# The output stores issued by SyncE instead of GpSimd, in a fused attention and stream-mixing kernel

## The chip, the cores and the metric

The kernel runs on one core of one Trainium2 chip. The metric is the device time of one execution in microseconds (us), as the median of several runs. Less is better.

The names of the engines: PE is TensorE (matrix products), DVE is VectorE, ACT is ScalarE, POOL is GpSimd. SP is SyncE, which computes nothing and only waits for semaphores and issues DMA transfers. POOL can issue DMAs too. A DMA that SP issues goes to the queue that the profile calls q1 (hardware_dynamic), one that POOL issues to q0 (software_dynamic). Both queues are served by the same 16 DMA engines.

## The reference

`x` is (8, 512, 2048) in float32: 8 batches, 512 rows (patches), 2048 columns. Cut to what is computed:

```
def layernorm(x): (x - mean) / sqrt(var + 1e-5)              # over the last axis, 2048
# 1. windowed attention, 8 heads of 32, windows of 128 columns; q and k from x, v from ctx
q, k = Wq @ xn + bq, Wk @ xn + bk;  val = Wv @ ctx + bv       # xn = layernorm(x)
o = softmax(q.T k / sqrt(32), masked) @ val;  out = (Wo @ gelu(o) + bo) * mask
x = x + tanh(g_xattn) * out
# 2. four streams of 512 columns, mixed by small per-row matrices
x1 = layernorm(x);  xr = x1 * rsqrt(mean(x1 * x1) + eps)
H_res  = sinkhorn(xr @ W_res.T + base, 50 iterations)         # 4 x 4 for every row
H_pre, H_post = softmax(xr @ W_pre.T + ..), softmax(xr @ W_post.T + ..)
H_res = (1 - g) * I + g * H_res
y = einsum(x1 streams, H_pre) @ W_branch                      # (rows, 512)
x = x + tanh(g_ffn) * (H_res mixes the four streams of x1 + y * H_post)
```

## The kernel before, in words

One loop counter `g` drives all engines. A step `g` is one attention unit (one window of 128 columns, 128 of the 256 attention channels). Eight steps make a chunk of 512 columns (`UPC` = 8), four chunks a batch (`UNITS` = 32 steps). There are 256 attention steps; the loop runs from -16 to 340, since the stream part of a batch follows its attention part by one to three batches' worth of steps. `G, r = chunk_step(g)` gives the chunk and the place in it. Each engine has its own program: it walks through the same `g` and does at each what tables of offsets say. The order on an engine is fixed by the code; engines meet only through semaphores.

The second part works in two stages. First, for each batch, 49 Sinkhorn iterations in scaling form, two iterations to a step: POOL multiplies `kp = ke * scale` (L526), DVE sums `kp` (L1134) and takes the reciprocal `sa` or `sv` (L1135), and so on back and forth. Then come the batch's four output tiles `t` (128 rows of 2048 columns each), eight steps apart, with step `TILE_AT[t]` as their origin. There are 32 tiles in all. For one tile:

- SP loads the 1 MB row block `x1t` (L385, `load_x1t`), seven steps ahead; there are two such buffers (even, odd). The load waits until the tile two before is complete, which DVE tells by `out_ready`.
- ACT makes the first product of `xpre` (L876), DVE adds the three others (L1167), PE transposes `xpre` (L675), ACT copies it (L884, `xpt`), and PE multiplies it by `W_branch` into bank `f` (L728, eight instructions).
- `otile` (128 x 4 x 512 float32, only one buffer) holds the output. ACT writes its first term for streams 0 and 1 (pair 0) at step -1 and for streams 2 and 3 (pair 1) at step +2 (L893, `first_out`). Before each it waits for `out_stored[pair]`: the store of that half for the tile before must have landed.
- DVE adds three stream products to pair 0 (L1179) at steps 0, 1, 2, then `y` from bank `f` to all four streams at step 3 (L1192, `add_y`, which waits between pair 0 and pair 1 for ACT's pair 1), then three stream products to pair 1 at steps 4, 6 and 7. `out_ready` goes up when pair 0 is complete and again when pair 1 is.
- The two halves are stored to DRAM, 512 KB each, at the end of step +4 and of step +8.

Until about 1660 us the attention of later batches runs beside the tiles of earlier ones. After that only Sinkhorn and tiles are left, and after about 1830 us only the last batch's last tiles.

What else SP does in a chunk of eight steps, in this order: the store of the sum `x1` to `x_dram` (1 MB, L378, waits for POOL's accumulating load to land, at r = 0), statistics loads `xs` (L373), 12 copies into `q_st` (L390, r = 3), more `xs`, the `x1t` load (r = 5), 12 copies into `k_st` and one row (L390, L435, r = 5), then `ctx_raw` (L359), a mask (L362) and `xc` (L356). What else POOL does: `kp`, normalising `xc` (L454), the low parts of `x` and `ctx` (L460, L465), and the accumulating loads into `x1c` (L474).

Of the kernel before, what the change touches and what calls it, by code (L numbers as in the profile page):

```python
# [12 lines left out]
B, D, S = 8, 512, 2048  # L13
# [3 lines left out]
DT = D // P  # L17
# [14 lines left out]
C = S // N  # L32
# [43 lines left out]
def chunk_step(g):  # L76
    return g // UPC, g % UPC


def at_step(g, lead, table):  # L80

    return [((g - r) // UPC - lead, i) for i, r in enumerate(table)
            if (g - r) % UPC == 0 and 0 <= (g - r) // UPC - lead < NG]


def ffn_at(g, e, width=1):

    f = (g - e) // UNITS - 1
    return [f] if (g - e) % UNITS == 0 and 0 <= f < B else []


def tiles_at(g, k):

    return [(f, t) for t in range(DT) for f in ffn_at(g, TILE_AT[t] + k)]


def sink_at(g):

    for f in range(B):
        n = g - UNITS * (f + 1) - SINK_AT  # L100
        if 0 <= n < len(SINK):
            return f, SINK[n]
    return None, (None, None)
# [56 lines left out]
def program(nc, x, ctx4, mask_bc, mask_t, gates, wq_t, bq, wk_t, bk, wv_t, bv, wo_t, bo, wf_t, base,  # L160
            w_branch, ident, stack_i, eye4, out):
    with ExitStack() as ctx:  # L162
        def sb(name, shape, dt=F32):
            return ctx.enter_context(nc.sbuf_tensor(name, shape, dt))
# [4 lines left out]
        def sem(name):  # L169
            return ctx.enter_context(nc.semaphore(name))  # L170
# [74 lines left out]
        otile = sb("otile", [P, N, C])  # L245
# [79 lines left out]
        out_ready = sem("out_ready")  # L325
        out_stored = [sem(f"out_stored{i}") for i in range(2)]
# [6 lines left out]
        outr = out.rearrange("b (t p) s -> b t p s", p=P)  # L333
# [20 lines left out]
        def _(sp):  # L354
# [10 lines left out]
            def load_maskt(b):  # L365
                sp.dma_start(maskt[:, b % 2, :], mask_t[b]).then_inc(maskt_loaded[b % 2], 16)
# [13 lines left out]
            def load_x1t(f, t):  # L380
# [3 lines left out]
                    sp.wait_ge(out_ready, 2 * (n - 1))  # L384
                sp.dma_start(x1t[n % 2][:], x1dr[f, :, t, :]).then_inc(x1t_loaded[n % 2], 16)  # L385

            def stack(G, dst, blocks):
                for r, (src, part) in enumerate(blocks):
                    for h in range(HPT):
                        sp.dma_start(dst[r * DH:(r + 1) * DH, G % 2, :, h, :],  # L390
                                     src[h * DH:(h + 1) * DH, part, :, :]).then_inc(stack_loaded[G % 2], 16)
# [24 lines left out]
            for g in range(FIRST, LAST):  # L416
# [11 lines left out]
                if r == 3 and 0 <= G + 1 < NG:  # L428
                    sp.wait_ge(qk_ready, 4 * (G + 1) + 2)
                    stack(G + 1, q_st, ((q_hl, 0), (q_hl, 1), (q_hl, 0)))  # L430
# [13 lines left out]
                if u == UPC + 6 and g >= 0 and b + 2 < B:  # L444
                    sp.wait_ge(bias_ready, b + 1)
                    load_maskt(b + 2)

        @block.gpsimd
        def _(pool):
            def norm_x(G, t):  # L450
                if t == 0:
                    pool.wait_ge(xc_loaded, 16 * (G + 1))
                    pool.wait_ge(xstat_ready, G // NC + 1)
                nc.gpsimd.tensor_scalar(xc[:, t, :], xc[:, t, :], ra[:, 2, t:t + 1], ra[:, 4, t:t + 1],  # L454
                                        ALU.mult, ALU.add).then_inc(x_norm, 1)

            def split_x(G, t):
                pool.wait_ge(x_norm, DT * G + t + 1)
                pool.wait_ge(x_hi, DT * G + t + 1)
                nc.gpsimd.tensor_tensor(x_hl[:, G % 2, 1, t, :], xc[:, t, :], x_hl[:, G % 2, 0, t, :], ALU.subtract  # L460
                                        ).then_inc(x_split, 1)

            def split_ctx(G, t):
                pool.wait_ge(ctx_hi, DT * G + t + 1)
                ins = nc.gpsimd.tensor_tensor(ctx_hl[:, 1, t, :], ctx_raw[:, t, :], ctx_hl[:, 0, t, :], ALU.subtract)  # L465
                if t == DT - 1:
                    ins.then_inc(ctx_split, 1)

            def add_x(G, h):
                pool.wait_ge(wo_read, DT * G + 2 * h + 2)  # L470
                if G:
                    pool.wait_ge(x1_added[h], 16 * G)
                b = G // NC
                pool.dma_start(x1c[:, 2 * h:2 * h + 2, :], xr[b, :, 2 * h:2 * h + 2, cols(G)],  # L474
                               accum_op=ALU.add).then_inc(x1_added[h], 16)

            def store(f, t, pair):
                pool.wait_ge(out_ready, f * (2 * DT) + 2 * t + pair + 1)
                half = slice(2 * pair * C, 2 * (pair + 1) * C)
                pool.dma_start(outr[f, t, :, half], otile[:, 2 * pair:2 * pair + 2, :].rearrange("p n c -> p (n c)")  # L480
                               ).then_inc(out_stored[pair], 16)

            cp = Chain(pool, pool_chain)

# [6 lines left out]
            def variance(b):  # L491
                pool.wait_ge(mv_a_ready, b + 1)
                nc.gpsimd.tensor_scalar(ra[:, 0, :], mv_a[:, :, 1], LN_EPS, None, ALU.add).then_inc(var_ready, 1)

            def xstat(b):
                pool.wait_ge(var_ready, b + 1)
                pool.wait_ge(rs_act, 2 * b + 2)
                newton(ra[:, 2, :], ra[:, 3, :], ra[:, 0, :], ra[:, 1, :])
                cp.link(nc.gpsimd.tensor_tensor(ra[:, 4, :], mv_a[:, :, 0], ra[:, 2, :], ALU.mult))
                nc.gpsimd.tensor_scalar(ra[:, 4, :], ra[:, 4, :], -1.0, None, ALU.mult).then_inc(xstat_ready, 1)  # L500

            def stat_b(f, part):
                r = rb[:, f % 2]
                if part == 0:
                    pool.wait_ge(mv_b_ready, f + 1)
                    cp.link(nc.gpsimd.tensor_scalar(r[:, 7, :], mv_b[:, :, 0], -1.0, None, ALU.mult))
                    nc.gpsimd.tensor_scalar(r[:, 0, :], mv_b[:, :, 1], LN_EPS, None, ALU.add).then_inc(rs_req, 1)
                elif part == 1:
                    pool.wait_ge(rs_req, 2 * f + 1)
                    pool.wait_ge(rs_done, 4 * f + 2)  # L510
                    newton(r[:, 3, :], r[:, 2, :], r[:, 0, :], r[:, 1, :])
                    cp.link(nc.gpsimd.tensor_tensor(r[:, 6, :], r[:, 7, :], r[:, 3, :], ALU.mult))
                    cp.link(nc.gpsimd.tensor_tensor(r[:, 4, :], r[:, 3, :], r[:, 3, :], ALU.mult))
                    cp.link(nc.gpsimd.tensor_tensor(r[:, 4, :], r[:, 4, :], mv_b[:, :, 1], ALU.mult))
                    nc.gpsimd.tensor_scalar(r[:, 4, :], r[:, 4, :], RMS_EPS, None, ALU.add).then_inc(rs_req, 1)
                else:
                    pool.wait_ge(rs_req, 2 * f + 2)
                    pool.wait_ge(rs_done, 4 * f + 4)
                    newton(r[:, 5, :], r[:, 2, :], r[:, 4, :], r[:, 1, :])
                    nc.gpsimd.tensor_tensor(r[:, 5, :], r[:, 5, :], r[:, 3, :], ALU.mult).then_inc(rb_ready, 1)  # L520
# [7 lines left out]
            def scale_at(f, its, part):  # L528
                it, half = its[part // 2], part % 2
                if (it, half) in SCALED:  # L530
                    scale(f, it, half)
# [5 lines left out]
            for g in range(FIRST, LAST):  # L537
                G, r = chunk_step(g)
                b, u = divmod(g, UNITS)
                f, its = sink_at(g)  # L540
                scale_at(f, its, 0)
                if g >= 0 and u == 17 and b + 1 < B:
                    variance(b + 1)
                if g >= 0 and u == 18 and b + 1 < B:
                    xstat(b + 1)
                for part in range(3):
                    for ready in ffn_at(g, STAT_AT + 1 + part):
                        stat_b(ready, part)
                for H, t in at_step(g, -2, LOW_X_AT):
                    split_x(H, t)  # L550
                scale_at(f, its, 1)
                for H, t in at_step(g, -2, NORM_AT):
                    norm_x(H, t)
                scale_at(f, its, 2)
                for H, t in at_step(g, -1, LOW_CTX_AT):
                    split_ctx(H, t)
                scale_at(f, its, 3)
                if 0 <= G - 1 < NG and r in (6, 7):
                    add_x(G - 1, r - 6)
                for done, t in tiles_at(g, 4):  # L560
                    store(done, t, 0)
                for done, t in tiles_at(g, 8):
                    store(done, t, 1)
            for pair in range(2):
                pool.wait_ge(out_stored[pair], 16 * DT * B)

        @block.tensor
        def _(pe):
# [753 lines left out]
```

## Time and profile before

| | |
|---|---|
| median of 3 runs | 1905.74 us (1904.44 to 1910.57) |
| the profiled execution's own time | 1909.33 us |
| its span | 1907.5 us |
| busy: PE, DVE, ACT, POOL | 1392.2 (73%), 1439.4 (75%), 945.7 (50%), 863.2 (45%) us |
| DMA queue q1 (issued by SP) | 230.41 MB, 39.2% of 16 engines' span |
| DMA queue q0 (issued by POOL) | 67.12 MB, 15.3% |
| stores of the output | 64 of 512 KB, issued by POOL at L480 |

How to read it: the span runs from the first to the last thing that the profile shows; the profiled execution's own time is 1.8 us longer. An engine's share of busy time is an average over stages that are limited by different things, so the stages are read one by one: the stretch with attention (to 1660 us), Sinkhorn with tiles (to 1830 us) and the last tiles (to 1907.5 us).

### The profile page before, as it was taken

The numbers are of one execution on the slowest core, as the hardware profiler recorded it, in microseconds if no ns is written. First come the engines' busy times: TensorE is split into PE (matmuls) and PEld (weight loads), VectorE is DVE, ScalarE is ACT, GpSimd is POOL, SyncE is SP. The second block draws the span as 40 slices with busy tenths as digits, with TensorE's granted clock in tenths as the row PEclk, the third lists the DMA queues.
The fourth block names the chain that finished last, engine by engine and source line by source line (L and its number), as shares of the span: only waits on it lengthen the run. The fifth ranks groups of instructions, "written<-read, shape, count | busy, mean of one in ns | idle before, by whom it ended". The sixth has DMA issues, their size and how long they took to land. (4 is left out here: it accounts for less than half of the span.)

```text
span 1907.5 us, 35318 instructions
## 1 busy us (share of the span) xinstructions
PE 1392.2 (73%) x12301; PEld 849.8 (45%) x12448; DVE 1439.4 (75%) x3684; ACT 945.7 (50%) x1889; POOL 863.2 (45%) x1461
## 2 busy tenths in 40 slices
PE   2788999888888787888888887878788875511323
PEld 0555556555544454445544554445455553200111
DVE  3344556767788888888888888888888888777787
ACT  2455676564655555554655555555555454210112
POOL 3433334555455545455465645554555523323310
PEclk9898999998999999998999999989999987755556
DMA  7456676566666665666666566665555543321123
GB/s 245 135 149 191 195 195 163 166 170 179 171 184 179 181 178 160 177 185 181 182 174 184 163 192 167 192 171 147 169 165 166 144 120 91 88 77 44 56 96 113
DMA packets 173984, 299.79 MB, mean 157 GB/s; under 512 B 23664, under 2 KB 74736, under 8 KB 169712
## 3 DMA queue, kind: packets, MB, share of 16 engines
q1 hardware_dynamic: 147184, 230.41, 39.2%
q0 software_dynamic: 26624, 67.12, 15.3%
q8 instruction: 100, 1.64, 0.4%
q14 instruction: 76, 0.62, 0.1%
HBM read 179.75 MB, written 67.11 MB: 129 GB/s over the span
## 5 line engine op out<-in xcount | busy, mean ns | idle before, releaser
L1134 DVE TENSOR_REDUCE ssum<-kp 128x16 f32<-128x64 f32 x768 | 181.7, 237 | 175.7 <-POOL kp L526 170.5
L526 POOL TENSOR_TENSOR kp<-ke,sv 128x64 f32<-128x64 f32 x376 | 183.9, 489 | 277.2 <-DVE sv L1135 274.4
L526 POOL TENSOR_TENSOR kp<-ke,sa 128x64 f32<-128x64 f32 x392 | 126.8, 323 | 329.1 <-DVE sa L1135 329.1
L805 ACT ACTIVATE probs<-st_ps,key_bias 128x512 f32<-128x512 f32 x256 | 174.5, 682 | 199.7 <-PE st_ps L702 193.9
L604 PE MATMUL pr<-x_hl,wk 128*128 128x512 bf16 x736 | 195.7, 422 | 66.0 <-DVE k_hl L982 65.2
L1002 DVE TENSOR_REDUCE negm<-s_ps 128x4 bf16<-128x512 f32 x256 | 167.7, 655 | 75.6 <-PE s_ps L688 73.0
L604 PE MATMUL pr<-x_hl,wq 128*128 128x512 bf16 x707 | 192.2, 420 | 44.5 <-POOL x_hl L460 38.3
L460 POOL TENSOR_TENSOR x_hl<-xc,x_hl 128x512 bf16<-128x512 f32 x128 | 157.4, 1230 | 136.9 <-ACT x_hl L773 136.5
L618 PE MATMUL pr<-wv,ctx_hl 128*128 128x256 bf16 x1536 | 188.6, 282 | 23.4 <-POOL ctx_hl L465 23.4
L465 POOL TENSOR_TENSOR ctx_hl<-ctx_raw,ctx_hl 128x512 bf16<-128x512 f32 x128 | 176.5, 1379 | 59.1 <-ACT ctx_hl L767 59.1
L688 PE MATMUL s_ps<-k_st,q_st 97*128 97x128 bf16 x1024 | 102.4, 223 | 111.4 <-DVE negm L1002 98.2
L631 PE MATMUL pr<-o_sb,wo 128*128 128x512 bf16 x714 | 176.6, 385 | 4.4 <-issue 1.5
L618 PEld LDWEIGHTS pr<-wv,ctx_hl 128*128 128x128 bf16 x1536 | 151.4, 102 | 56.7 <-issue 35.6
L688 PEld LDWEIGHTS s_ps<-k_st,q_st 97*128 97x128 bf16 x1024 | 73.6, 99 | 188.8 <-DVE negm L1002 123.0
L700 PE MATMUL st_ps<-q_st,k_st 96*128 96x128 bf16 x1024 | 149.8, 223 | 7.3 <-ACT probs L805 4.4
L604 PEld LDWEIGHTS pr<-x_hl,wk 128*128 128x128 bf16 x768 | 79.6, 106 | 160.1 <-DVE k_hl L982 64.1
L702 PE MATMUL st_ps<-id_bf,negm 128*128 128x128 bf16 x1024 | 149.3, 223 | 0.0
L1010 DVE TENSOR_TENSOR o_sb<-av_ps,rden 128x128 f32<-128x128 f32 x256 | 70.4, 275 | 104.3 <-ACT rden L814 103.9
L715 PE MATMUL av_ps<-probs,v_t 128*32 128x128 f32 x2048 | 112.2, 291 | 42.8 <-DVE o_sb L1010 42.4
L728 PE MATMUL f<-wb,xpt 128*128 128x512 f32 x256 | 135.8, 680 | 8.5 <-ACT xpt L884 8.5
L604 PEld LDWEIGHTS pr<-x_hl,wq 128*128 128x128 bf16 x768 | 76.2, 106 | 145.7 <-issue 46.9
L675 PE MATMUL pr<-id_sb,xpre 128*128 128x128 f32 x128 | 24.0, 320 | 160.2 <-DVE xpre L1167 160.2
(140 smaller groups left out, 3079.2 us busy)
## 6 DMA issues: line engine op xcount, KB each, us to landing
xs<-in_dram SPq DMA_DIRECT2D x128, 256.0 KB, 3.9
xc<-in_dram SPq DMA_DIRECT2D x32, 1024.0 KB, 5.9
ctx_raw<-in_dram SPq DMA_DIRECT2D x32, 1024.0 KB, 5.1
x1c<-in_dram POOLq DMA_DIRECT2D x64, 512.0 KB, 6.0
x_dram<-x1c SPq DMA_DIRECT2D x32, 1024.0 KB, 5.4
out_dram<-otile POOLq DMA_DIRECT2D x64, 512.0 KB, 3.5
q_st<-q_hl SPq DMA_DIRECT2D x384, 64.0 KB
k_st<-k_hl SPq DMA_DIRECT2D x384, 64.0 KB
```

Of the source, the lines that this page charges most:

```text
L460: nc.gpsimd.tensor_tensor(x_hl[:, G % 2, 1, t, :], xc[:, t, :], x_hl[:, G % 2, 0, t, :], ALU.subtract).then_inc(x_split, 1)
L465: ins = nc.gpsimd.tensor_tensor(ctx_hl[:, 1, t, :], ctx_raw[:, t, :], ctx_hl[:, 0, t, :], ALU.subtract)
L526: nc.gpsimd.tensor_tensor(kp[:], ke[:], v, ALU.mult).then_inc(kp_made, 1)
L604: ins = nc.tensor.matmul(bank(what)[:], w[:, a, t, i * P:(i + 1) * P], x_hl[:, G % 2, m, t, :], start=(t == 0 and a + m == 0), stop=(t == ...
L618: ins = nc.tensor.matmul(bank(what)[:, j * E:(j + 1) * E], ctx_hl[:, a, t, win], wv[:, m, t, :], start=(t == 0 and a + m == 0), stop=(t == ...
L631: ins = nc.tensor.matmul(bank(what)[:], wo[:, a, et, t * P:(t + 1) * P], o_part(G, et, m), start=(et == 0 and a + m == 0), stop=(et == ET ...
L688: ins = nc.tensor.matmul(s_ps[:, h * W:(h + 1) * W], q_st[0:ROWS + 1, G % 2, et, h, win], k_st[0:ROWS + 1, G % 2, et, h, win], start=True, ...
L700: nc.tensor.matmul(part, k_st[0:ROWS, G % 2, et, h, win], q_st[0:ROWS, G % 2, et, h, win], start=True, stop=False)
L702: ins = nc.tensor.matmul(part, negm[:, k % 2, h:h + 1].broadcast_to([P, P]), id_bf[:], start=False, stop=True)
L805: nc.scalar.activation(probs[:, k % 2, :], st_ps[:], ACT.Exp, bias=key_bias[:, b % 2, w:w + 1], scale=SCALE).then_inc(exp_done, 1)
L1002: nc.vector.tensor_reduce(negm[:, k % 2, :], s_ps[:].rearrange("p (h j) -> p h j", h=HPT), AX.X, ALU.max, negate=True).then_inc(max_done, 1)
L1134: cf.link(nc.vector.tensor_reduce(s_t, k, AX.X, ALU.add))
```

## The change

The function `store` moves from POOL's program to SP's, with the same waits and the same transfer; so do the two calls for each step, which stand at the end of the step's body in both programs, and the last wait for all the stores.

```
         @block.sync
+            def store(f, t, pair):
+                sp.wait_ge(out_ready, f * (2 * DT) + 2 * t + pair + 1)
+                half = slice(2 * pair * C, 2 * (pair + 1) * C)
+                sp.dma_start(outr[f, t, :, half], otile[:, 2 * pair:2 * pair + 2, :].rearrange("p n c -> p (n c)")
+                               ).then_inc(out_stored[pair], 16)
...
+                for done, t in tiles_at(g, 4):
+                    store(done, t, 0)
+                for done, t in tiles_at(g, 8):
+                    store(done, t, 1)
+            for pair in range(2):
+                sp.wait_ge(out_stored[pair], 16 * DT * B)
...
         @block.gpsimd
-            def store(f, t, pair):
-                pool.wait_ge(out_ready, f * (2 * DT) + 2 * t + pair + 1)
-                half = slice(2 * pair * C, 2 * (pair + 1) * C)
-                pool.dma_start(outr[f, t, :, half], otile[:, 2 * pair:2 * pair + 2, :].rearrange("p n c -> p (n c)")
-                               ).then_inc(out_stored[pair], 16)
...
-                for done, t in tiles_at(g, 4):
-                    store(done, t, 0)
-                for done, t in tiles_at(g, 8):
-                    store(done, t, 1)
-            for pair in range(2):
-                pool.wait_ge(out_stored[pair], 16 * DT * B)
```

What SP issues in one chunk of the middle of the program, after the change (here L390 is the new store, and the copies into `q_st` and `k_st`, which were L390, are L396; in brackets what the instruction waits for):

```order
L378 DMA x_dram<-x1c 128x4x512 [waits x1_added1,x1_added0]
L390 DMA out_dram<-otile 128x1024 [waits out_ready]
L373 DMA xs<-in_dram 128x512 [waits xs_taken]
L396 DMA q_st<-q_hl 32x2x512 [waits qk_ready]
L396 DMA q_st<-q_hl 32x2x512 x11
L373 DMA xs<-in_dram 128x512 [waits xs_taken] x3
L390 DMA out_dram<-otile 128x1024 [waits out_ready]
L385 DMA x1t_even<-x_dram 128x2048 [waits out_ready,x1_stored]
L396 DMA k_st<-k_hl 32x2x512 [waits qk_ready]
L396 DMA k_st<-k_hl 32x2x512 x11
```

The two stores of a chunk have come in: pair 0 behind the `x_dram` store and ahead of `q_st`, pair 1 directly ahead of the `x1t` load. The other rows stand in the order of before.

The end of SP's program before: the `x1t` loads of the last tiles, each of which waits for the tile two before, and nothing between them.

```order
L385 DMA x1t_even<-x_dram 128x2048 [waits out_ready,x1_stored]
L385 DMA x1t_odd<-x_dram 128x2048 [waits out_ready,x1_stored]
L385 DMA x1t_even<-x_dram 128x2048 [waits out_ready,x1_stored]
L385 DMA x1t_odd<-x_dram 128x2048 [waits out_ready,x1_stored]
L162 UNCONDITIONAL_BRANCH
```

The same place now, with the stores of the last tiles:

```order
L390 DMA out_dram<-otile 128x1024 [waits out_ready] x2
L385 DMA x1t_even<-x_dram 128x2048 [waits out_ready,x1_stored]
L390 DMA out_dram<-otile 128x1024 [waits out_ready] x2
L385 DMA x1t_odd<-x_dram 128x2048 [waits out_ready,x1_stored]
L390 DMA out_dram<-otile 128x1024 [waits out_ready] x4
L162 UNCONDITIONAL_BRANCH [waits out_stored1,out_stored0]
```

The second store of each row of two is the pair 1 of a tile; the load behind it waits for the same count of `out_ready`.

The end of POOL's program before; now the stores and the wait for them are gone, and it ends behind the last `kp`.

```order
L526 TENSOR_TENSOR kp<-ke,sa 128x64 [waits scale_made]
L526 TENSOR_TENSOR kp<-ke,sv 128x64 [waits scale_made]
L526 TENSOR_TENSOR kp<-ke,sa 128x64 [waits scale_made]
L480 DMA out_dram<-otile 128x1024 [waits out_ready] x10
L162 UNCONDITIONAL_BRANCH [waits out_stored1,out_stored0]
```

## Rows read from the trace of the kernel before

**Rows 1.** Windows, by stage: busy us of each engine, granted TensorE clock, DMA share, GB/s

```profile
480.00:1660.00 1180.00, 939.40 (x8403) 572.96 (x8509) 993.41 (x2583) 649.95 (x1300) 595.22 (x1000) 0.92 0.59 166
1830.00:1907.50 77.50, 28.34 (x48) 12.07 (x48) 60.95 (x89) 16.20 (x23) 5.40 (x10) 0.63 0.31 108
```

**Rows 2.** Chain that ended last, in order of time: start, us, what

```profile
1839.96 0.29 issue
1840.25 7.03 DMA out_dram<-otile
```

**Rows 3.** Timeline from 1839 us: start, us, engine, instructions, [idle before <-releaser]

```profile
1839.09 6.68 PE L728 MATMUL f<-wb,xpt 128*128 128x512 f32 x8 [0.69 <-ACT xpt L884]
1840.02 0.32 SPq L385 DMA_DIRECT2D x1t_odd<-x_dram  x1
1840.25 0.53 POOL L480 DMA_DIRECT2D out_dram<-otile  x1 [7.31 <-DVE otile L1179]
1845.88 1.41 DVE L1192 SCALAR_TENSOR_TENSOR otile<-f,post,otile 128x512 f32<-128x512 f32 x2 [1.71 <-PE f L728]
1847.30 1.52 ACT L893 ACTIVATE otile<-x1t_even,ccon,cmat 128x512 f32<-128x512 f32 x2 [6.86 <-DMA out_dram<-otile]
1848.73 0.80 ACT L876 ACTIVATE xpre<-x1t_odd,rb,pre 128x512 f32<-128x512 f32 x1
1848.86 1.41 DVE L1192 SCALAR_TENSOR_TENSOR otile<-f,post,otile 128x512 f32<-128x512 f32 x2 [1.56 <-ACT otile L893]
...
1856.00 6.76 PE L728 MATMUL f<-wb,xpt 128*128 128x512 f32 x8 [0.69 <-ACT xpt L884]
...
1872.81 5.19 PE L728 MATMUL f<-wb,xpt 128*128 128x512 f32 x8 [0.69 <-ACT xpt L884]
...
1889.56 5.35 PE L728 MATMUL f<-wb,xpt 128*128 128x512 f32 x8 [0.69 <-ACT xpt L884]
```

**Rows 4.** Waits of DVE from 1660 us: total us, times, longest

```profile
DVE otile L1192 <- ACT otile L893: 5.8, 3, 2.9
```

**Rows 5.** DMA issues of 1856.5 to 1858 us: median us from issue to landing

```profile
x1t_even<-x_dram SPq DMA_DIRECT2D x1, 1024.0 KB, 5.9
out_dram<-otile POOLq DMA_DIRECT2D x1, 512.0 KB, 6.9
```

**Rows 6.** DMA issues of 1812.5 to 1820.5 us, each alone on the queues

```profile
x1t_even<-x_dram SPq DMA_DIRECT2D x1, 1024.0 KB, 4.8
out_dram<-otile POOLq DMA_DIRECT2D x1, 512.0 KB, 2.9
```

**Rows 7.** DMA issues of the whole program (page, part 6)

```profile
x_dram<-x1c SPq DMA_DIRECT2D x32, 1024.0 KB, 5.4
x1t_even<-x_dram SPq DMA_DIRECT2D x16, 1024.0 KB, 7.5
```

**Rows 8.** Windows of L728 alone: PE, PEld busy, granted clock, DMA share, GB/s

```profile
1872.80:1875.00 2.20, 2.19 (x3) 1.16 (x4) 0.50 0.48 45
1876.30:1878.00 1.70, 1.70 (x4) 0.39 (x3) 1.00 1.05 376
```

**Rows 9.** Tile out_dram from 500 to 1670 us: count, ns min/median/max

```profile
L480 POOL DMA_DIRECT2D out_dram<-otile x45: 600/618/1042, 531.9 to 1655.0; - x45
```

**Rows 10.** Timeline of POOL: what follows the store of 558.66, and another store

```profile
560.29 0.29 POOL L526 TENSOR_TENSOR kp<-ke,sv 128x64 f32<-128x64 f32 x1 [1.01 <-DVE sv L1135]
...
1743.93 0.61 POOL L480 DMA_DIRECT2D out_dram<-otile  x1 [0.15 <-issue]
1744.56 0.31 POOL L526 TENSOR_TENSOR kp<-ke,sv 128x64 f32<-128x64 f32 x1
```

**Rows 11.** Waits of SP from 500 to 1660 us: total us, times, longest

```profile
SPq L390 <- DVE q_hl L982: 147.2, 20, 8.7
SPq L390 <- DVE k_hl L982: 40.6, 20, 3.4
```

**Rows 12.** Waits of PE over the program: total us, times, longest

```profile
PE s_ps L688 <- DMA k_st<-neg_row: 13.1, 2, 7.4
```

## The prediction

> **What bounds the kernel now.** I read the busy shares by stage first. In the stretch with attention DVE is busy 993 of 1180 us, POOL 595 and ACT 650; in the last 77.5 us it is 61 [rows 1]. So the long stretch is set by DVE and by its exchanges with POOL, ACT and PE, and idle time on POOL is plentiful there. Next I followed the chain that ended last, from its end backwards. Up to about 1830 us it alternates between DVE and POOL (Sinkhorn). From there it takes another form: in the last tiles a DMA of 7.03 us stands on it, the store of the output [rows 2]. The timeline around it tells why. DVE completes pair 1 of one tile at 1839.96. POOL issues that half's store at 1840.25, and it lands at 1847.28 [rows 2]. `otile` has one buffer, so ACT may write the first term of pair 1 of the next tile only then (1847.30, after 6.86 us of waiting). By then PE has long delivered `y` (1845.77) and DVE has added it to pair 0 (1845.88 to 1847.29). DVE then waits 1.56 us for ACT before it can go on with pair 1 [rows 3]. This happens in three tiles and adds up to 5.8 us, the longest 2.9 [rows 4]. It is the only place where I find a store of the output that holds DVE up.
>
> **Why the store takes 7 us there.** Its landing takes 6.9 us beside an `x1t` load of 1 MB that SP issued 0.22 us before it [rows 5], but 2.9 us alone [rows 6]. Both were released by the same event, the completion of pair 1. SP simply reacts sooner (1840.02 against 1840.25), so the load goes first and the store's last bytes come in with the load's [rows 3].
>
> **What the change does there.** SP now issues the pair-1 store and only then the `x1t` load, on one queue. The store should start at 1840.03 (SP follows DVE by 0.07 where POOL follows by 0.29) and the load one issue later, 0.32 us. The landing time of a 512 KB store from SP is not in the trace. From below, I take the 2.9 us of POOL's store alone; from above, the 5.4 us of SP's store of 1 MB, twice the size [rows 6, 7]. I take 3.5: SP's load of 1 MB alone needs 4.8, POOL's 512 KB 2.9 [rows 6], and half of the 1 MB is worth about 1.3 us at the 376 GB/s that the engines reach when loaded [rows 8]. ACT can then write pair 1 from about 1843.6 to 1845.2, before `y` is there, and DVE's 1.56 us of waiting goes.
>
> The rule that speaks against this is that both transfers use the same 16 DMA engines either way. The Trainium skill, page "DMA: Bandwidth & Descriptors", section "Issuing engines are not separate DMA queues", says that transfers from different issuers interleave on the same engines and that the choice of issuer saves only sequencer time. By it alone the store would still land beside the load and only 0.22 us would be won per tile; that is the first rival below. The same page, "Queues, rings and completion order", says that descriptors of one ring are consumed in order and that a completion increment lands only after the earlier writes of its DMA engine, whatever the queue. By that rule the load that goes first holds back the store's completion now, and will not when the store goes first. The trace agrees with this second rule as far as it goes: the load lands after 5.9 us, the store after 6.9, not after 2.9 [rows 5].
>
> **What is late next.** Once the store is out of the way, the cycle of the last tiles goes through PE: `y` arrives, DVE adds it to both pairs, adds one product to pair 1, makes `xpre`, PE transposes, ACT copies, PE multiplies. From the start of DVE's pair-1 `y` to the start of the next `f` product it is 1856.00 - 1848.86 = 7.14 us; from the end of `f` to the start of pair 1, without the wait, 0.11 + 1.42 = 1.53. The new cycle is 8.67 us plus the duration of `f`. The old one was 16.91, 16.81 and 16.75 us (starts 1839.09, 1856.00, 1872.81, 1889.56), 50.47 in all [rows 3]. With the three durations of `f` of this trace (6.68, 6.76, 5.19) the new ones are 26.01 + 18.63 = 44.64: 5.83 us less, the same as the wait seen before [rows 4]. But the duration of `f` depends on the moment at which TensorE's clock goes from 0.50 (1.2 GHz) to 1.00 (2.4 GHz) within the group [rows 8], and this moment will fall elsewhere once the cycles are shorter. The mean of the four groups, 6.68, 6.76, 5.19 and 5.35, is 6.0 [rows 3]. Before, the cycle did not depend on `f` at all; now each microsecond of it counts. With 6.0 the three cycles take 44.0 us, **6.5 less**. If all are as slow as 6.76 the gain is 4.2, if all are 5.19 it is 8.9. I take 6.5, the mean.
>
> Two covers have to hold. The store must land before about the end of `f`, since ACT needs 1.52 us and DVE's pair-0 `y` lasts 1.41: with an `f` of 5.19 that leaves 4.2 us from the issue, with 6.7 it leaves 5.7. At 3.5 both hold; at the upper bound of 5.4 a tile with a fast `f` loses 1.2 again. And the `x1t` load, issued 1.3 us after the start of `f`, must land and ACT must make 0.8 us of first product before DVE begins with `xpre`, which is 0.11 + 2.73 + 1.45 after the end of `f`, 9.5 us after its start in the fast case. At 5.9 us, what it takes beside a store today [rows 5], there are 1.5 us left; at the 7.5 that it needs in traffic [rows 7] nothing is left, and nothing is lost.
>
> **The other stores on POOL.** POOL spends 0.62 us on each of 45 stores before 1670 us [rows 9], 28 us in all. Behind nearly all of them it then waits for DVE, as at 560.29, where `kp` starts after 1.01 us of idling [rows 10]: earlier readiness gives nothing. Looking through the 53 stores before 1832 us, 41 are followed by such idling. Behind twelve `kp` follows without it; in nine of these it starts 0.73 us behind the start of the store, which is when its scale is ready, and in three directly behind the issue, 0.62 to 0.64 behind the store's start. There the store may have held `kp` by about 0.1 us (at 1743.93 to 1744.56, [rows 10], against the beat of 0.96 from one `kp` to the next of its kind). That is **0.3** gained; the bounds are 0 and, if all twelve were held, 1.2.
>
> **The new work on SP.** 64 issues of about 0.35 us, with two waits for `out_ready` in each tile. Behind the pair-0 store stand `xs` and the 12 `q_st` copies. SP waits in all 20 chunks for `q_hl`, 147.2 / 20 = 7.4 us each, which covers the issue, and the pair-0 half was completed before SP is through with the `x_dram` store. Behind the pair-1 store stand the `x1t` load, which waits for the same count anyway, and the 12 `k_st` copies, with 40.6 / 20 = 2.0 us of waiting each [rows 11]. PE waits for `k_st` only twice in the program, both outside the stretch in question [rows 12]. So this costs nothing; without that cover each tile would cost an issue, 0.4 us. The `x1t` load is delayed by the same 0.3 to 0.4 us and is wanted a chunk later.
>
> **The end.** SP should issue the last store 0.2 us sooner than POOL, which is the difference of their two reactions at 1840 us [rows 3]. Against that stands the landing, 3.5 taken for 2.9 now. Together **0.4 lost**, between 0.2 gained (2.9) and 2.3 lost (5.4). The page named above gives the first byte of a DMA from SP as about 0.6 us and from GpSimd as about 1 us; by that an estimate of the end would be 0.4 better than mine, and no row here has a 512 KB store from SP.
>
> **The sum.** 6.5 + 0.3 - 0.4 = 6.4 us off the profiled execution's 1909.33, which gives 1902.9. That execution was 3.6 us above the median of the runs, and the time to predict is a median: 1905.74 - 6.4 = **1899.3**.
>
> **Rivals.**
> - *The transfers still interleave.* The store of SP lands with the load as it does now, since the same 16 engines carry both. For it: 6.9 us against 2.9 depends on company alone [rows 5, 6]. Against it: the order of the two is now reversed, on one queue. Only 0.22 us of issue in three tiles, 0.7, and the 0.3 on POOL would be gained, less the end: 1905.7 - 0.6 = 1905.1. A milder form is that the landing takes around 5 us, or that the load's later landing becomes the new wait (ACT at L876), and half of the gain is lost: 1902.5.
> - *The freed POOL counts in the long stretch.* 28 us of POOL time; if a quarter of it reached DVE, 7 us more would go: 1892. Against it is POOL's idling behind 41 stores [rows 10].
> - *SP becomes late (slower than before).* The place is the pair-1 store in the stretch with attention. If its issue is held up, for want of room in the queue behind `q_st` and `xs`, the `k_st` copies start later, and past 2.0 us [rows 11] the first scores of each chunk wait. It decides from the point where a chunk's `k_st` lands after its first score; every further microsecond costs 20 chunks one each. At 0.7 us that is +14, on top of the forecast: 1913. Against it: the copies are issued by 563 us in the chunk at 554 and are wanted about 17 us later.
>
> **How the numbers follow.** Forecast (most of the wait goes, 1893.5 to 1902): 0.60. Interleaving or half of the gain: 0.25. Freed POOL: 0.07. SP late: 0.08. A measurement of this kernel can tell about 0.3% from no change, which is 5.7 us: below 1900.0 is faster, above 1911.5 slower. The forecast sits near that line: with `f` between its bounds and the landing between its bounds it is on the fast side in about eight of ten. So faster 0.60 x 0.8 + 0.07 = 0.55; the rest of the forecast, the interleaving and part of the late SP is 0.12 + 0.25 + 0.03 = 0.40; slower is the rest of the late SP, 0.05. The range reaches from the fast end of `f` with something from POOL, 1894, to the interleaving case, 1905.
>
> **What the profile would show.** Right: the chain in the last tiles has no store on it but the final one; the landing of the stores there is 3 to 4 us; DVE's wait for ACT at L1192 is gone and its wait for PE's `f` has grown; cycles of 8.7 us plus `f`; 1660 us is reached at the same time as before, within 1 us. Wrong: stores from SP that land after more than 5 us in the last tiles; a wait of ACT for `x1t` before `xpre`; PE waiting for `k_st` in the middle; or a stretch up to 1660 us that has changed by several microseconds, for which I have no term.

## The result, and the profile after

The changed kernel takes **1891.2 us** (median, 1889.32 to 1898.57, 8 runs) where the kernel before takes 1904.64 in the same set (1902.55 to 1910.57, 8 runs): a ratio of 0.993, 95% interval [0.9914, 0.9947], which is 13.3 us less (10.1 to 16.4). That is twice the 6.4 us of the prediction, and 1891.2 lies below its range of 1894 to 1905. Two more sets of runs of the changed kernel gave 0.9946 and 0.992 (experiments e0 and e11 below), which is 10.3 and 15.3 us less. The profiled execution of the changed kernel took 1890.67 us, its span is 1888.8.

The stages answer to [rows 1]. Columns as there.

```profile
480.00:1660.00 1180.00, 938.04 (x8416) 572.96 (x8521) 995.18 (x2590) 651.97 (x1304) 569.18 (x961) 0.92 0.60 165
1830.00:1889.00 59.00, 25.11 (x48) 11.09 (x48) 53.87 (x78) 16.54 (x23) 0.00 (x0) 0.73 0.37 134
```

In the long stretch POOL is relieved of 26 us and DVE is as busy as it was. The last stage has changed in kind: before, DVE was busy 61 of 77.5 us, now it is 54 of 59.

The chain that ended last, in the second of the cycles between two `f` products (before: a DMA of 7.03 us, [rows 2]):

```profile
1845.92 5.21 PE f L729 x8
1851.23 2.74 DVE otile L1193 x4
1854.03 0.63 issue
1854.66 0.76 DVE otile L1180
1855.44 0.76 DVE xpre L1168
...
1857.92 1.10 PE pr L676 x4
1859.04 0.61 ACT xpt L885
1859.69 5.15 PE f L729 x8
```

No store stands on it any more. `f`, `y` on all four streams in one go (2.74), a stream product, `xpre`, transposition, copy, next `f`: 13.77 us.

The timeline of the first of these cycles, which answers to [rows 3]:

```profile
1832.05 5.31 PE L729 MATMUL f<-wb,xpt 128*128 128x512 f32 x8 [0.69 <-ACT xpt L885]
1832.93 0.33 SPq L390 DMA_DIRECT2D out_dram<-otile  x1
1833.36 0.38 SPq L385 DMA_DIRECT2D x1t_odd<-x_dram  x1
1835.88 1.52 ACT L894 ACTIVATE otile<-x1t_even,ccon,cmat 128x512 f32<-128x512 f32 x2 [2.48 <-DMA out_dram<-otile]
1837.46 2.73 DVE L1193 SCALAR_TENSOR_TENSOR otile<-f,post,otile 128x512 f32<-128x512 f32 x4 [0.34 <-PE f L729]
1839.20 0.81 ACT L877 ACTIVATE xpre<-x1t_odd,rb,pre 128x512 f32<-128x512 f32 x1 [1.80 <-DMA x1t_odd<-x_dram]
```

The store goes first and the load 0.43 us later. ACT writes pair 1 at 1835.88, before `f` is done (1837.36); DVE does both pairs of `y` without a stop. ACT now waits 1.80 us for `x1t`, which it did not before (the wait is new, and the prediction had listed it as a sign of being wrong). It costs nothing here: ACT has its product at 1840.01, before DVE reaches `xpre` at 1841.68. The issues of 1832 to 1834.5 us with their landings, answering to [rows 5]:

```profile
x1t_odd<-x_dram SPq DMA_DIRECT2D x1, 1024.0 KB, 5.8
out_dram<-otile SPq DMA_DIRECT2D x1, 512.0 KB, 2.9
```

The load takes as long as before, the store 2.9 instead of 6.9 us. In the two cycles that follow the store takes 3.4 and 3.0 us. DVE's waits from 1660 us, answering to [rows 4]: first the wait for `f` in the kernel before, which stands beside the 5.8 us for ACT there, then that of the changed kernel. The 5.8 us for ACT are gone:

```profile
DVE otile L1192 <- PE f L728: 4.1, 4, 1.8
```

```profile
DVE otile L1193 <- PE f L729: 0.7, 3, 0.3
```

So both of DVE's waits shrank, 5.8 and 4.1 us to nothing and 0.7. The prediction expected the second to grow.

Busy time in the three cycles between the four `f` products; first the kernel before, then the changed one. Columns as in [rows 1]:

```profile
1839.09:1856.00 16.91, 7.77 (x13) 3.24 (x13) 13.39 (x20) 4.23 (x7) 1.07 (x2) 0.60 0.38 125
1856.00:1872.81 16.81, 7.85 (x13) 3.24 (x13) 13.39 (x20) 4.23 (x7) 1.07 (x2) 0.60 0.37 125
1872.81:1889.56 16.75, 6.28 (x12) 2.79 (x13) 13.38 (x20) 4.22 (x7) 1.07 (x2) 0.70 0.39 125
```

```profile
1832.05:1845.92 13.87, 6.39 (x12) 2.80 (x12) 13.29 (x20) 4.33 (x7) 0.00 (x0) 0.75 0.43 152
1845.92:1859.69 13.77, 6.29 (x12) 2.80 (x12) 13.30 (x20) 4.34 (x7) 0.00 (x0) 0.75 0.44 154
1859.69:1873.40 13.71, 6.23 (x13) 2.76 (x13) 13.29 (x20) 4.34 (x7) 0.00 (x0) 0.75 0.42 153
```

DVE does the same 13.3 us of work in each, and the time around it went from 3.5 to 0.5 us. The three cycles together are 41.35 us instead of 50.47: **9.1 us** less. TensorE's granted clock is 0.75 instead of 0.60 to 0.70.

The end. Before, DVE is through at 1902.10 (1900.68 plus 1.42), POOL issues the last store at 1902.39, it lands 2.9 us later, at 1905.3, and the span goes on to 1907.5. The last issue before, then DVE's end and the last issue after:

```profile
1902.39 0.53 POOL L480 DMA_DIRECT2D out_dram<-otile  x1 [5.13 <-DVE otile L1179]
```

```profile
1884.28 1.42 DVE L1180 SCALAR_TENSOR_TENSOR otile<-x1t_odd,cmat,otile 128x512 f32<-128x512 f32 x2
1885.72 0.33 SPq L390 DMA_DIRECT2D out_dram<-otile  x1
```

The issue comes 0.02 us behind DVE, the landing takes 2.6 us (1888.3), and the span ends at 1888.8. From DVE's last instruction to the end it is 3.1 instead of 5.4 us: **2.3 us** less, of which 0.3 is the issue, 0.3 the landing and 1.7 what follows the landing.

SP has room for its new work. Its waits from 500 to 1660 us, answering to [rows 11], and the stores in that part:

```profile
SPq L396 <- DVE q_hl L983: 137.6, 20, 8.4
SPq L396 <- DVE k_hl L983: 32.1, 19, 2.5
```

```profile
L390 SPq DMA_DIRECT2D out_dram<-otile x46: 338/497/1057, 530.5 to 1662.9; - x46
```

The moved stores land later in this stretch, after 5.5 us in the median where it was 3.8; one wait of ACT, 2.0 us, is put down to them. SP's two waits shrank by 9.6 and 8.5 us, about the cost of issuing, and stayed well above zero. PE waits for `k_st` twice in the whole program, as before (11.5 us instead of 13.1, [rows 12]).

9.1 and 2.3 make 11.4 of the measured 13.3. The two profiles differ by more, 18.7 us of span; the rest of that lies ahead of the first of the four `f` products (1839.09 against 1832.05). Single executions can't size it: this mark stands at 1831.75 to 1835.81 in five profiles of kernels whose POOL has no work at all in the places of the stores, and at 1832.03, 1832.19, 1839.09 and 1839.12 in four in which POOL issues most or all of them. The same holds at 1660 us, where the prediction allowed for 1 us of change and named more as a sign of being wrong. The `f` product nearest to it starts at 1661.87 before and at 1655.21 after, but at 1654.95 in e1, where POOL issues every store up to there, and at 1657.91 and 1658.40 in e0 and e11, which are the changed kernel again.

### The profile page after: what moved, and what is told of

Same layout as the page of the kernel before. It is cut to its first block and busy times, and to the rows that moved or that the text cites. A ratio compares the mean times of both kernels' runs of the same rounds, so it can differ in the third digit from the quotient of the medians.

```text
span 1888.8 us, 35318 instructions
## 1 busy us (share of the span) xinstructions
PE 1383.0 (73%) x12301; PEld 848.2 (45%) x12448; DVE 1437.9 (76%) x3684; ACT 945.7 (50%) x1889; POOL 824.0 (44%) x1397
## 5 line engine op out<-in xcount | busy, mean ns | idle before, releaser
L605 PE MATMUL pr<-x_hl,wq 128*128 128x512 bf16 x707 | 187.0, 411 | 44.8 <-POOL x_hl L473 38.1
L729 PE MATMUL f<-wb,xpt 128*128 128x512 f32 x256 | 132.0, 664 | 8.5 <-ACT xpt L885 8.5
```

The lines of the kernel that those rows point to most:

```text
L605: ins = nc.tensor.matmul(bank(what)[:], w[:, a, t, i * P:(i + 1) * P], x_hl[:, G % 2, m, t, :], start=(t == 0 and a + m == 0), stop=(t == ...
L729: ins = nc.tensor.matmul(f1[:], xpt[:, j * P:(j + 1) * P], wb[:, j, :], start=(j == 0), stop=(j == C // P - 1))
```

## The experiments

Theory A, the prediction's: in the last tiles the order decides in which the pair-1 store and the `x1t` load are issued. Rival B: who issues decides, or POOL's freed time in the long stretch. It also had to be explained why the gain was twice as large as forecast. In the kernels that split the stores between SP and POOL each queue has semaphores of its own, and ACT waits for the last one of its pair.

**e1 and e2: one part of the stores each.**

```diff
+            def on_sp(f, t, pair):
+                return f == B - 1          # e1;  e2: f < B - 1
```

> Stores of the last batch's four tiles are issued by SyncE, those of the other 28 tiles by GpSimd as before. Theory A (the time went in the last tiles and at the very end): three cycles of about 13.8 us in place of 16.8, the end of the span about 3 us behind the last DVE instruction in place of 5.4, together 11 to 12 us below the kernel before: a ratio of 0.994. Theory B (it is mainly GpSimd's freed time in the long stretch): most of the gain is missing, 3 to 6 us below before.

> The opposite part: stores of the first 28 tiles by SyncE, those of the last batch by GpSimd. Theory A: the last cycles and the end stay as before (16.8 us, 5.4 us); only some 1.5 us are gained in the long stretch, where chunks were 0.12 to 0.16 us shorter here and there: 1903. Theory B: 7 us or more are gained, 1897 or less.

Both expectations give the last batch three cycles. It has two. In the first of the three cycles the pair-1 store that ACT needs is that of the last tile of the batch before, which is POOL's in e1 and SP's in e2. That is also why e1 gained less than the 11 to 12 us expected. Measured: e1 0.9954 [0.9934, 0.9975], e2 0.9972 [0.9958, 0.9985]. The `f` starts of e1, then the DMA pieces on the chain of e1, then those of e2:

```profile
1832.03 5.12 PE L751 MATMUL f<-wb,xpt 128*128 128x512 f32 x8 [0.69 <-ACT xpt L907]
1849.00 5.17 PE L751 MATMUL f<-wb,xpt 128*128 128x512 f32 x8 [0.69 <-ACT xpt L907]
1862.74 5.13 PE L751 MATMUL f<-wb,xpt 128*128 128x512 f32 x8 [0.69 <-ACT xpt L907]
1876.43 5.11 PE L751 MATMUL f<-wb,xpt 128*128 128x512 f32 x8 [0.69 <-ACT xpt L907]
```

```profile
1833.18 7.10 DMA out_dram<-otile
```

```profile
1846.93 6.97 DMA out_dram<-otile
1863.77 6.89 DMA out_dram<-otile
```

In e1 the cycles are 16.97, 13.74, 13.69; in e2 13.87, 16.85, 16.76. Each cycle is long exactly where its store is POOL's. The terms then add up: e1 saves 6.1 us in two cycles and 2.3 at the end, 8.4, and measured 8.8 (1907.33 times 0.0046; 5 to 13); e2 saves 3.0 in one cycle and 0.5 at the end (4.9 instead of 5.4 us), and measured 5.3 (3 to 8). The 1.8 left over in e2 is what the stores of the long stretch may be worth, but with that interval it can be anything from nothing to 4.5.

**e3: the last store and the final wait alone.**

```diff
+            def on_sp(f, t, pair):
+                return f == B - 1 and t == DT - 1 and pair == 1
```

> Only the very last of the 64 stores, and the wait for all of them at the end, are SyncE's. If the end of the span is a term of its own, as comparing the two profiles says (5.39 us from the last DVE instruction to the end before, 3.10 after), 2.3 us are gained, ratio 0.9988. If the shorter end in that profile was chance or came from fewer transfers in flight, nothing is gained. The cycles of the last tiles stay at 16.8 us.

Ratio 0.9995 [0.9981, 1.0009]: no difference that the runs can tell, and 2.3 us lies inside the interval. The runs alone would also allow that nothing is gained; the shorter end rests on the profile. The end of the chain of e3, then its last issue:

```profile
1902.00 0.75 DVE otile L1202
1902.75 0.66 DVEq L162
```

```profile
1903.44 0.34 SPq L398 DMA_DIRECT2D out_dram<-otile  x1
```

DVE is through at 1903.41, the span ends at 1906.5: 3.1 us. Where SP issues and awaits the last store the end takes 3.1 us (changed kernel, e1, e3, e4), where POOL does it takes 5.4 (before, e5) or 4.9 (e2). Whether issuing or awaiting makes the difference wasn't separated.

**e4: everything on SP, but the load first.** Made from the changed kernel:

```diff
-                for done, t in tiles_at(g, 8):
+                for done, t in tiles_at(g, 9):
                     store(done, t, 1)
+            store(B - 1, DT - 1, 1)
```

> All stores by SyncE, but in each tile the x1t load is issued ahead of the store of pair 1, on the same queue. If the order of the two is what counts, the store lands after 6 to 7 us in the last tiles, the cycles are 16.5 to 16.9 us again and some 9 us of the gain go; the end of the span stays short (3 us). If it is the queue that counts and not the order, the store lands after 3 to 4 us as in the changed kernel and the time is that of the changed kernel, 1891.

Ratio 0.9983 [0.9969, 0.9997], 3.2 us less than before instead of 13. The DMA pieces on its chain:

```profile
1833.43 6.84 DMA out_dram<-otile
1850.30 6.61 DMA out_dram<-otile
1866.95 6.75 DMA out_dram<-otile
```

With SP issuing both and the load 0.38 us ahead, the store takes 6.6 to 6.8 us again, DVE waits 7.9 us for ACT, and the cycles are 16.87, 16.64 and 16.79. So with one issuer and one queue the order is what counts. What e4 keeps is the end (2.3) and POOL's freed time: together 3.2 us (0.6 to 5.9), which leaves 0.9 for POOL, with zero and 3.6 both inside the interval.

**e5: the kernel before, with the order turned on the two queues.** POOL sets a flag behind the issue of the store, and SP's last two loads wait for it:

```diff
+                if f == B - 1 and t >= 2:
+                    sp.wait_ge(issued, t - 1)
...
+                if f == B - 1 and pair:
+                    pool.memset(flag[:, t:t + 1], 0.0).then_inc(issued, 1)
```

> The kernel before, all stores on GpSimd's queue, but the x1t loads of the last batch's third and fourth tile wait until GpSimd has issued the store of pair 1 (a one-column memset behind it tells so). If the order of the two transfers is what counts, whichever queue, the last two cycles are 13.8 to 15.3 us long and the store lands after about 3 us; the first cycle stays at 16.9, and the kernel is 3 to 6 us faster than before. If the hardware queue itself is what counts, the store still lands after 6 to 7 us and nothing is gained.

Ratio 0.9985 [0.9973, 0.9998]. The issues of 1848 to 1852 us:

```profile
x1t_even<-x_dram SPq DMA_DIRECT2D x1, 1024.0 KB, 6.0
out_dram<-otile POOLq DMA_DIRECT2D x1, 512.0 KB, 3.8
```

The first cycle, left as it was, takes 16.68 us, the two others 14.36 and 14.00. GpSimd's queue serves nearly as well, if its store goes first: 3.8 us here and 3.3 us in the next cycle, with the load 0.72 behind it. DVE waits for ACT once, 2.4 us in the first cycle, and not in the two others. The two cycles gain 5.2 us in the profile. The runs show less: 2.9 (0.4 to 5.1) by the ratio, and medians of 1904.2 and 1904.41, hardly apart (one of the twelve executions of e5 took 3479.81 us and isn't in the ratio). Where the rest goes is open; that the wait goes is read from the trace.

**e0 and e11: the changed kernel again**, unedited, beside e5 to e7 and beside e8 to e10.

> The changed kernel once more, beside the other three of this set: 11 to 15 us below the kernel before, f products of 5.1 to 5.3 us in the last tiles, cycles of 13.7 to 13.9.

> The changed kernel once more, unedited, as the measure for e8, e9 and e10 on the same chip. Every theory: the ratio of 0.993 to 0.995 to the kernel before, cycles of the last tiles of 13.7 to 14.6 us, 3.1 us from DVE's last instruction to the end.

e0: 1895.59 us, 0.9946 [0.9934, 0.9958]. e11: 1892.09 us, 0.992 [0.9898, 0.9942]. The `f` products of e0:

```profile
1835.38 6.01 PE L729 MATMUL f<-wb,xpt 128*128 128x512 f32 x8 [0.69 <-ACT xpt L885]
1849.95 5.55 PE L729 MATMUL f<-wb,xpt 128*128 128x512 f32 x8 [0.69 <-ACT xpt L885]
1864.08 5.32 PE L729 MATMUL f<-wb,xpt 128*128 128x512 f32 x8 [0.69 <-ACT xpt L885]
1877.96 5.21 PE L729 MATMUL f<-wb,xpt 128*128 128x512 f32 x8 [0.69 <-ACT xpt L885]
```

Its cycles are 14.57, 14.13 and 13.88: each 8.6 us plus its `f`. In e11 `f` goes from 5.91 to 5.19 in the same way. Both are above what was expected, `f` of 5.1 to 5.3. So the cycles' part of the gain is 7.9 to 9.1 us, by how fast `f` is at the start.

The traces of all kernels show a pattern in `f` (us, the four groups in order, and the cycles between them):

| kernel | `f` | cycles |
|---|---|---|
| before | 6.68, 6.76, 5.19, 5.35 | 16.91, 16.81, 16.75 |
| e3 | 6.16, 6.23, 6.40, 6.41 | 16.93, 16.72, 17.06 |
| e4 | 5.34, 5.44, 5.65, 5.79 | 16.87, 16.64, 16.79 |
| e1 | 5.12, 5.17, 5.13, 5.11 | 16.97, 13.74, 13.69 |
| e5 | 5.59, 5.79, 5.44, 5.26 | 16.68, 14.36, 14.00 |
| e0 | 6.01, 5.55, 5.32, 5.21 | 14.57, 14.13, 13.88 |
| changed | 5.31, 5.20, 5.14, 5.11 | 13.87, 13.77, 13.71 |

In the thirteen traces other than e7's, `f` is shorter than the one before behind each of the 26 cycles of 13.7 to 15.2 us. Behind 12 of the 13 cycles of 16.6 to 17.1 us it is longer, by 0.01 to 0.21; the thirteenth is the fall from 6.76 to 5.19 in the kernel before. What differs inside a group is how long TensorE stays at the lower clock: in the `f` of 5.20 us the granted clock is 0.50 (1.2 GHz) from 1846.0 to 1848.6 and 1.00 (2.4 GHz) from 1849.5 to 1851.0, in the `f` of 6.68 it is 0.54 from 1839.2 to 1845.6. Why this moment moves with the length of the cycle no run here shows, and the first `f` is 5.12 us in e1 without any short cycle ahead of it.

**e7: TensorE kept at work in the last tiles.** Twenty products into the idle bank `s_ps` behind each `f`, which the output doesn't use:

```diff
+                if f == B - 1 and t < DT - 1:
+                    for i in range(20):
+                        nc.tensor.matmul(s_ps[:], id_bf[:], wo[:, 0, 0, :], start=True, stop=True)
```

> The changed kernel, with 20 bf16 products (128x512, into a bank that is free then) behind each f product of the last batch but the last, so that TensorE's clock is high when the next one starts. Theory A (VectorE is the bound of the new cycle, 13.6 of 13.8 us busy): f products of 3.5 to 4.5 us, but the cycles are only 0.1 to 0.3 us shorter. Theory B (PE's f product is the bound, as the prediction had it): the cycles fall to 12.2 to 13.2 us, 3 us gained.

1892.74 us, 0.9938 [0.9923, 0.9952]: not to be told from e0. Its first two cycles:

```profile
1831.75:1845.70 13.95, 10.74 (x31) 4.58 (x33) 12.83 (x20) 4.33 (x7) 0.00 (x0) 0.84 0.42 151
1845.70:1859.27 13.57, 10.29 (x32) 4.41 (x33) 13.29 (x20) 4.34 (x7) 0.00 (x0) 0.87 0.44 155
```

The expected `f` of 3.5 to 4.5 us did not come: it is 5.84 in the first cycle and 5.40 in the others. What is faster is the transposition behind `xpre`, 0.63 instead of 1.09 us, so that the next `f` starts sooner. DVE waits for `f` only once, 0.9 us in the first cycle. At 13.57 us the cycle is therefore DVE's own: 13.29 busy and no wait. The changed kernel with 13.7 to 13.9 is within 0.3 us of that floor.

**e6, e8, e9, e10: what POOL's time is worth.** The changed kernel, with this at each of the 64 places where POOL had a store, which keeps POOL busy or waiting there without issuing anything:

```diff
+            def fill(f, t, pair):
+                n = f * (2 * DT) + 2 * t + pair
+                pool.wait_ge(out_ready, n + 1)             # e6, e8, e10
+                if n:
+                    pool.wait_ge(filled, n)                # e6, e9, e10
+                nc.gpsimd.tensor_scalar(fill_sb[:], fill_sb[:], 1.0, None, ALU.mult).then_inc(filled, 1)
```

`fill_sb` is 128x384 in e6 and e9 and 128x160 in e10; e8 has the first wait alone.

> The changed kernel, with GpSimd kept as busy as before: at each of the 64 places it waits for out_ready and then multiplies a 128x384 tile of its own by 1 (about 0.6 us). Theory A (GpSimd's 0.62 us per store delayed kp in the long stretch, by small amounts that also move PE's groups to another clock): the stretch up to the last tiles is as long as before, 2 to 5 us longer than in the changed kernel; the last cycles and the end stay short: 1894 to 1896. Theory B (GpSimd's time never mattered, the difference there is chance): the same time as the changed kernel within 1 us.

> The changed kernel, with GpSimd waiting for `out_ready` at each of the 64 places where a store stood, and doing nothing there. If what GpSimd gives back in the long stretch is its blocking (it may not run ahead past an unfinished tile), this costs about as much as e6 did, 4 to 5 us over the changed kernel. If it is the occupation by the issue, it costs nothing: within 1 us of the changed kernel. I expect the second, 0.7.

> e6 without the wait for `out_ready`: at each of the 64 places GpSimd only multiplies (1.23 us each in e6, 79 us in all). Occupation theory: 4 to 5 us over the changed kernel, as e6. Blocking theory: within 1 us of it. I expect the first, 0.65. Freed time that is worth nothing (my prediction's view): both e8 and e9 within 1 us.

> e6 with a smaller multiply (128x160 instead of 128x384), an estimated 0.6 us each, which is what a store's issue took on GpSimd. If the cost goes with the time occupied, it is half of what e6 showed: 2.0 to 2.5 us over the changed kernel, the part of the gain that e1's and e2's terms leave for the long stretch. If it is the mere presence of one more instruction and its wait, it is that of e6, 4 to 5 us.

| kernel | POOL at each place | us, median | ratio to before |
|---|---|---|---|
| e6 | wait, 1.23 us of work | 1900.42 | 0.9969 [0.9955, 0.9983] |
| e9 | 1.25 us of work | 1902.45 | 0.9968 [0.9953, 0.9984] |
| e10 | wait, 0.67 us of work | 1893.32 | 0.9926 [0.9903, 0.995] |
| e8 | wait | 1893.37 | 0.9926 [0.9903, 0.9948] |
| e11 (e8 to e10's set) | nothing | 1892.09 | 0.992 [0.9898, 0.9942] |
| e0 (e6's set) | nothing | 1895.59 | 0.9946 [0.9934, 0.9958] |

The work of e9 and that of e10 in POOL's groups:

```profile
L496 POOL TENSOR_SCALAR fill_sb<-fill_sb 128x384 f32<-128x384 f32 x64 | 79.7, 1246 | 0.8
```

```profile
L497 POOL TENSOR_SCALAR fill_sb<-fill_sb 128x160 f32<-128x160 f32 x64 | 42.6, 665 | 85.9 <-DVE otile L1195 57.7 <-DVE otile L1208 28.1
```

The multiply of e6 was expected to take 0.6 us and took twice that; e10 has the shorter one. The blocking is worth nothing that can be measured (1.3 us). 80 us of work costs 4.8 us in the set of e6, where the intervals overlap, and 10.4 in that of e9, where they don't touch. The ratios of e6 and e9 to the kernel before are nearly the same, 0.9969 and 0.9968; it is the unedited kernel that came out at 0.9946 in one set and 0.992 in the other. 43 us of work, a little more than the issues of the stores took (64 of 0.53 to 0.62 us), costs 1.2 us, which is no difference the runs can tell. It doesn't go in proportion; 2.0 to 2.5 were expected.

For Sinkhorn with tiles the traces show why. A multiply and the `kp` behind it, in e10 and in e9:

```profile
1743.91 0.61 POOL L497 TENSOR_SCALAR fill_sb<-fill_sb 128x160 f32<-128x160 f32 x1
1744.61 0.30 POOL L542 TENSOR_TENSOR kp<-ke,sv 128x64 f32<-128x64 f32 x1
```

```profile
1743.88 1.17 POOL L496 TENSOR_SCALAR fill_sb<-fill_sb 128x384 f32<-128x384 f32 x1
1745.02 0.30 POOL L541 TENSOR_TENSOR kp<-ke,sv 128x64 f32<-128x64 f32 x1
```

In e10 this `kp` starts 0.96 us behind the `kp` before it (1743.65), which is the beat without any work between; in e9 it starts 1.41 behind (1743.61). The short multiply fits into POOL's idle time, as the issue of a store did [rows 10], and the long one doesn't. From the `f` product nearest 1660 us to the first of the last four it is 180.0 us in e9 and 180.3 in e6, and 176.6 to 177.7 in the twelve other traces, with stores on POOL or without. So in this stretch POOL's relief can't be told from nothing. For all stores ahead of the last tiles e2, e4 and e10 leave 1.8, 0.9 and 1.2 us, none clear of zero.

## Why the prediction fell short

- **The mechanism of the wait held.** The prediction named the wait (ACT for the store, DVE for ACT), its cause (the load issued 0.2 us ahead) and its end (the store goes first). e4 and e5 show the cause from both sides: on one queue with the order turned the wait is back, on two queues with the order turned it goes. The size did not follow: 6.4 us were forecast and 13.3 measured, outside the range. The rule of the Trainium skill's "DMA: Bandwidth & Descriptors", section "Issuing engines are not separate DMA queues", was weighed as a reason for a small gain. For the landing of a store beside a load the traces agree with it: the issuer doesn't decide (6.6 to 6.8 us in e4, 3.3 and 3.8 in e5). But it does not speak of the order that comes with a change of issuer, and at the end of the program the issuer did make a difference (e3).
- **The landing** was taken as 3.5 us; 2.9, 3.4 and 3.0 were measured in the cycles and 2.6 at the end. In the cycles the difference changed nothing, since both values are covered.
- **The size of `f` is the first step that failed.** The cycle is, as predicted (8.67), a constant plus `f`: 13.87 - 5.31, 13.77 - 5.20 and 13.71 - 5.14 give 8.56 and 8.57. But the prediction took for `f` the 6.0 us that is the mean of four groups in a kernel whose cycles last 17 us, two of them slow and two fast. In the changed kernel the three that count are 5.31, 5.20 and 5.14, and in e0 they start at 6.01 and fall to 5.32. The term of 6.5 us measured 9.1 (7.9 in e0, 8.1 in e11); 2.4 of the difference is `f`, 0.3 the constant. The same shows in DVE's waits: beside the 5.8 us for ACT the wait for `f` fell from 4.1 to 0.7, 9.2 us together, where at an `f` of 6.01, the first of e0, DVE still waits 1.0 us. The fast bound of 8.9 came close, but how fast `f` is when the last tiles begin differs from trace to trace (5.12 to 6.62 us) and was not to be foreseen from one. Why is open.
- **The end is the second.** The prediction compared the reactions and the landings of the last store, and not what comes behind it. The landing of 2.9 us from 1902.39 ends at 1905.3, the span at 1907.5. Those 2.2 us stood in the trace and had no term; with SP they are 0.5. A term of -0.4 was +2.3 in the profiles, which the runs of e3 neither confirm nor exclude.
- **POOL's stores ahead of the last tiles** were given 0.3 us. e2, e4 and e10 leave 1.8, 0.9 and 1.2, each with zero in its interval, and the upper ends of e2 and e4 are 4.5 and 3.6. The rival of 7 us isn't borne out. Whether it is 0.3 or 2 or somewhat more stays open.
- **SP** had room, as predicted: its waits for `q_hl` and `k_hl` paid for the issues.
- **The base** moved as well: 1905.74 was the median before, and 1904.64 in the set of the result. That is 1.1 us of the 8.1 by which 1899.3 was off.

Summed up: 9.1 + 2.3, and an open part for POOL, against 13.3 (10.1 to 16.4) measured; in e0 7.9 + 2.3 against 10.3. The order of the transfers is shown by experiments. The shorter end is shown in the profiles alone, and the size of POOL's part is not shown.

## What to carry to other kernels

Where two transfers are released by the same event, issue first the one that somebody waits for; here it cost nothing, and it mattered more than who issues. When a wait goes and a group of products becomes part of the cycle, don't size it by the mean of a trace with other cycles: here its duration fell from one short cycle to the next and rose from one long cycle to the next. Give both bounds, and look for the next engine's floor (here DVE's 13.3 us of work). Follow the end of the program to the last instant of the span, past the last landing.

## What the runs showed of the hardware

- A 512 KB store lands after 2.6 us (SP) or 2.9 us (POOL) alone; after 2.9 to 3.5 us with a 1 MB load issued 0.43 us behind it on SP's queue; after 3.3 to 3.8 us with that load 0.72 behind it on the other queue; after 6.6 to 7.2 us with the load 0.2 to 0.4 ahead, on one queue or two. The load takes 5.5 to 6.3 us in all these cases.
- From the landing of the last store to the end of the span it is 2.2 us (before, e5) or 1.7 us (e2) where GpSimd issued and awaits it and 0.5 us where SyncE does.
- A multiply of 128x384 float32 took POOL 1.23 to 1.25 us, one of 128x160 0.67 us; between two `kp` of Sinkhorn 0.61 us of it passed without a delay, 1.17 us held the next `kp` by 0.45 us.
- With twenty small products behind each `f` the granted clock of the cycle rose from 0.75 to 0.87, and yet `f` itself took 5.40 us instead of 5.14 to 5.20. Why stays open.
